# Cross attention and its hand-over to the expert layer: the last output products in four banks, the first two experts' weights prepared early, and the first expert started by halves

## The chip, the cores and the metric

The kernel runs on one NeuronCore of one Trainium2 chip. The metric is the device time of one execution in microseconds; given are the median of three timed runs and one execution under the hardware profiler. The engines are PE (matrix products and transposes), DVE (vector), ACT (scalar, activation functions), POOL (GpSimd) and SP, which here only issues DMAs.

## The reference, cut to what matters

Two decoder layers on x of shape (4, 256, 256). The change lies in the last two of six steps: cross attention of layer 1 and its mixture of experts.

```
x = x + _L1_xattn_ref(_layernorm(x), ctx, Wq, Wk, Wv, Wo, q_norm_w, k_norm_w, pos, itok)   # 16 heads, 4 key heads, 128 wide
    probs = softmax(q @ k.T * SCALE); attn = probs @ v; return attn.reshape(.., 16 * 128) @ Wo.T
x = x + _L1_ffn_ref(_layernorm(x), w_gate, wi_0, wi_1, wo)                                 # 8 experts, top 2, M = 128
    inter = silu(xf @ wi_0[e]) * (xf @ wi_1[e]); out = inter @ wo[e], weighted by softmax of the two top logits
```

## The kernel before, in words

Every stage is a block of five programs, one for each engine, written out in full and tied together by semaphores. Between stages all engines meet at a barrier (L68), which also clears the stage's semaphores.

**Cross attention** (`cross_stream`) is one long stream. A group g is one batch row and one key head with its four query heads; there are 16 groups (`GROUPS`), and each has 30 slots (`STEPS`), one for each tile of 128 keys and each half of the 512 query columns. In a slot PE computes the scores of one such tile (`score`, L1866, three bf16 products of the high and low halves of q and k), DVE adds the row shift and takes them out of the bank (`lower`, L2096), ACT takes the exponential (L1939), POOL adds it into `acc` for the softmax sum (L2033), and PE multiplies it with v two slots later (`weigh`, L1879, f32). The scores use banks 0 and 1 in turn, the weighted sums banks 2 and 3. Projections of the groups to come, maxima of scores (`piece`), and transposes fill the rest of the slots. In the last group, which has no successor, only the chain just named is left.

What is left of a group when its 30 slots are over is done in the slots of the next: ACT and DVE split the weighted sums into a bf16 high and low half (`att`, L1983 and L2138), PE sums `acc` over the partitions by a product with ones (`side` of kind "sum", L1895, in two halves of four columns of bank 6), DVE takes the reciprocals (L2149), and for each of the four heads PE makes the output product (`project_out`, L1905, six products of 128x256 into bank 6) and DVE scales it and adds it to x (`add_out`, L2159, two instructions). `sides_in` and `outs_in` are the tables that say in which slot each of these comes, and `bank6_before` says how many readers of bank 6 a writer has to wait for. Since all of them share bank 6, each product waits for the additions before it. `SLOTS` runs 14 slots past the last group, in which only this tail is left.

**The experts** (`expert_ffn`, tiles named `moe_...`) begin after the barrier. DVE normalises x (L86 to L2289, with a power on POOL, L2270), PE transposes it in four batches (L2391), ACT copies each out twice (bf16 high half L2354, f32 L2355), DVE makes the low half (L2294). PE then makes the up products of expert 0 in two halves n of 512 tokens (`up`, L2404, 24 instructions), the gate's logits (L2412), and then for each expert the next one's up products and this one's down products (L2426). The weights come in four pairs of experts by DMA into f32 tiles; ACT makes the high halves (`pair_high`, L2346 and L2347), POOL the low halves (`pair_rest`, L2266 and L2267).

`ctx_t` and `in_t` are the f32 context of one batch row and its two bf16 halves; they are allocated in `decoder` under the name `row0` (in the trace `row_ctx_t`, `row_in_t_hi`, `row_in_t_lo`). The last context row is loaded into `ctx_t`, and split, during group 10; `in_t` is read by the projections of keys and values until those of group 15 are made.

## Time and profile before

| | |
|---|---|
| median of 3 runs (lowest, highest) | 1791.28 us (1777.04, 1791.42) |
| the profiled execution, its time | 1775.8 us |
| its span, first to last instruction | 1774.0 us |
| mean granted clock of PE | 0.952 of full speed |
| busy: PE, DVE, ACT, POOL | 1585.2, 1334.4, 783.6, 1166.7 us |

The stages lie in the span as follows: cross attention's stream from 447.6 to 1676.2 us, the experts from 1677.5 us to the end. A busy share is time in which an engine works on some instruction, so the shares of several engines overlap. The granted clock is what PE's throttle allowed: 1.00 is 2.4 GHz, 0.50 is 1.2 GHz, and a value in between is a stretch that holds both.

### The profile page before, as it was taken

Reading aid. Unit: us, or ns where it says so; the run is one execution under the profiler, and the core shown is the slowest. Engines: PE = TensorE matmul, PEld = TensorE weight load, DVE = VectorE, ACT = ScalarE, POOL = GpSimd, SP = SyncE. Lnnn points to the kernel's source line nnn. Section 1 sums busy time; section 2 is a strip of 40 time slices with the busy share of each in tenths; the row PEclk is TensorE's granted clock in tenths of the full one; section 3 lists DMA queues with packets and bytes.
Section 4 is the critical chain, followed back from the end, with each engine's and each line's share of the span. In section 5 each row is a group of like instructions: output and inputs, shape, how many; then the busy total and the mean of one; then the engine's idle time right before and its main releaser. Section 6 shows DMA issues by size and latency. Waiting matters only on the chain. (4 is left out here: it accounts for less than half of the span.)

```text
span 1774.0 us, 26948 instructions
## 1 busy us (share of the span) xinstructions
PE 1585.2 (89%) x8690; PEld 912.3 (51%) x8690; DVE 1334.4 (75%) x2674; ACT 783.6 (44%) x1915; POOL 1166.7 (66%) x1088
## 2 busy tenths in 40 slices
PE   7697795776779999999999999899999999999797
PEld 4475463533534555554555555455555555544344
DVE  7675567778777888889788787877878778776454
ACT  2363564652435444443545444444444444433242
POOL 3663560132657799787779978678987787866442
PEclk9799897988989999999999999999999999999789
DMA  2001821010100000100000100000000000000110
GB/s 71 1 2 44 271 81 48 1 68 0 50 0 13 1 13 1 50 1 1 1 1 1 38 1 1 1 1 1 1 1 1 1 1 1 1 1 1 35 37 25
DMA packets 28530, 38.55 MB, mean 22 GB/s; under 512 B 4836, under 2 KB 24808, under 8 KB 28392
## 3 DMA queue, kind: packets, MB, share of 16 engines
q1 hardware_dynamic: 28392, 36.83, 6.3%
q8 instruction: 72, 1.18, 0.3%
q14 instruction: 66, 0.54, 0.1%
HBM read 35.78 MB, written 1.05 MB: 21 GB/s over the span
## 5 line engine op out<-in xcount | busy, mean ns | idle before, releaser
L2033 POOL TENSOR_TENSOR stream_acc<-stream_acc,stream_p 128x512 f32<-128x512 f32 x448 | 571.9, 1281 | 181.3 <-ACT stream_p L1939 180.0
L1939 ACT ACTIVATE stream_p<-stream_lowered 128x512 f32<-128x512 f32 (+1 forms) x480 | 302.7, 631 | 632.6 <-DVE stream_lowered L2096 596.4
L1879 PE MATMUL stream_banks<-stream_p,stream_v 128*128 128x512 f32 (+1 forms) x960 | 490.7, 593 | 4.5 <-ACT stream_p L1939 4.5
L2096 DVE TENSOR_TENSOR stream_lowered<-stream_banks,stream_shift_all 128x512 f32<-128x512 f32 (+1 forms) x480 | 329.2, 686 | 105.9 <-PE stream_banks L1866 93.1
L2103 DVE TENSOR_REDUCE stream_tops<-stream_banks 128x1 f32<-128x512 f32 (+1 forms) x512 | 324.4, 636 | 93.5 <-PE stream_banks L1852 92.4
L1879 PEld LDWEIGHTS stream_banks<-stream_p,stream_v 128*128 128x128 f32 (+1 forms) x960 | 182.5, 191 | 75.8 <-ACT stream_p L1939 7.0
L1852 PE MATMUL stream_banks<-stream_k_t_hi,stream_q_t_hi 128*128 128x512 bf16 (+1 forms) x512 | 185.4, 363 | 20.6 <-DVE stream_tops L2103 19.5
L1866 PE MATMUL stream_banks<-stream_q_t_hi,stream_k_t_hi 128*128 128x512 bf16 (+1 forms) x480 | 183.6, 382 | 0.0
L1866 PE MATMUL stream_banks<-stream_q_t_hi,stream_k_t_lo 128*128 128x512 bf16 (+1 forms) x480 | 182.6, 380 | 0.0
L1866 PE MATMUL stream_banks<-stream_q_t_lo,stream_k_t_hi 128*128 128x512 bf16 (+1 forms) x480 | 182.6, 380 | 0.0
L2040 POOL TENSOR_TENSOR stream_by_cos<-stream_by_cos,stream_by_sin 128x256 f32<-128x256 f32 x192 | 133.5, 718 | 35.0 <-DVE stream_by_sin L2129 34.9
L1852 PEld LDWEIGHTS stream_banks<-stream_k_t_hi,stream_q_t_hi 128*128 128x128 bf16 x512 | 50.1, 98 | 157.5 <-issue 154.8
L1949 ACT ACTIVATE stream_squares<-stream_banks 128x128 bf16<-128x128 f32 x368 | 95.4, 267 | 26.1 <-PE stream_banks L1798 26.1
L2046 POOL TENSOR_TENSOR stream_rms<-stream_var,cross_half 128x4 f32<-128x4 f32 x96 | 105.6, 1100 | 0.0
L2051 POOL TENSOR_TENSOR stream_normed<-stream_by_cos,stream_rms 128x512 f32<-128x512 f32 x96 | 97.2, 1012 | 11.3 <-PE stream_banks L1840 3.9
L1798 PEld LDWEIGHTS stream_banks<-early_w_kv_hi,row_in_t_hi 128*128 128x128 bf16 x416 | 40.7, 98 | 81.5 <-issue 56.8
L1798 PE MATMUL stream_banks<-early_w_kv_hi,row_in_t_hi 128*128 128x256 bf16 x416 | 80.3, 275 | 2.3 <-DVE stream_by_sin L2129 2.3
L1798 PE MATMUL stream_banks<-early_w_kv_hi,row_in_t_lo 128*128 128x256 bf16 x416 | 80.4, 275 | 0.0
L1798 PE MATMUL stream_banks<-early_w_kv_lo,row_in_t_hi 128*128 128x256 bf16 x416 | 80.4, 275 | 0.0
L1866 PEld LDWEIGHTS stream_banks<-stream_q_t_hi,stream_k_t_lo 128*128 128x128 bf16 (+1 forms) x480 | 47.5, 99 | 56.7 <-issue 0.8
L1949 ACT ACTIVATION_READ_ACCUMULATOR stream_squares<-stream_banks 128x1 f32 x368 | 73.4, 199 | 0.0
L2159 DVE SCALAR_TENSOR_TENSOR model_x<-stream_banks,stream_inv,model_x 128x256 f32<-128x256 f32 x128 | 56.0, 478 | 21.6 <-PE stream_banks L1905 21.6
(403 smaller groups left out, 2900.1 us busy)
## 6 DMA issues: line engine op xcount, KB each, us to landing
memory_raw_t<-in_ctx_t SPq DMA_DIRECT2D x4, 1601.0 KB, 8.1
row_ctx_t<-in_ctx_t SPq DMA_DIRECT2D x4, 1601.0 KB, 7.4
memory_raw<-in_ctx SPq DMA_DIRECT2D x4, 1536.0 KB
early_raw<-in_L_xattn_Wq SPq DMA_DIRECT2D x4, 512.0 KB, 3.9
stream_raw_o<-in_L_xattn_Wo SPq DMA_DIRECT2D x4, 512.0 KB, 3.7
moe_raw_up<-in_L_ffn_wi SPq DMA_DIRECT2D x8, 256.0 KB, 4.6
model_x<-in_x SPq DMA_DIRECT2D x1, 1024.0 KB, 5.5
ffn_raw_fc<-in_L_ffn_w_fc SPq DMA_DIRECT2D x1, 1024.0 KB, 5.0
```

What stands on the lines that cost most here:

```text
L1798: last = nc.tensor.matmul(out, rows, moving(two, c), start=(n == 0), stop=(n == 3 * DC - 1))
L1852: nc.tensor.matmul(ps[:, piece_bank(item), 0:n], q_t[0][:, g % 3, h, q * P:(q + 1) * P], k_t[0][:, g % 2, s:s + n], start=True, stop=True) ...
L1866: last = nc.tensor.matmul(ps[0:r, step % 2, :], k_t[one][:, g % 2, t * P:t * P + r], q_t[two][:, g % 3, 2 * n:2 * n + 2, :], start=(one == ...
L1879: nc.tensor.matmul(ps[:, 2 + n, :], v[0:r, g % 2, t, :], p32[0:r, step % 4, :], start=(t == 0), stop=(t == KT - 1)).then_inc(weighed, 1)
L1939: nc.scalar.activation(p32[0:r, step % 4, :], lowered[0:r, step % 3, :], ACT.Exp, scale=SCALE).then_inc(p32_ready, 1)
L1949: last = nc.scalar.activation(squares[:, h, :], heads[:, h - some.start, :], ACT.Square, accum_out=ss[:, u % 2, h:h + 1])
L2033: nc.gpsimd.tensor_tensor(acc[0:r, g % 2, cols], acc[0:r, g % 2, cols], p32[0:r, step % 4, :], ALU.add).then_inc(acc_ready, 1)
L2040: last = nc.gpsimd.tensor_tensor(by_cos[:, u % 2, 0:n, to], by_cos[:, u % 2, 0:n, to], by_sin[:, u % 2, 0:n, of], ALU.add)
L2046: nc.gpsimd.tensor_tensor(rms[:, u % 2, 0:n], var[:, u % 2, 0:n], half[:, 0:n], ALU.pow).then_inc(rms_ready, 1)
L2051: nc.gpsimd.tensor_tensor(normed[:, 0:n], by_cos[:, u % 2, 0:n], bcast(rms[:, u % 2, 0:n], 2, HD), ALU.mult).then_inc(normed_ready, 1)
L2096: nc.vector.tensor_tensor(lowered[0:r, step % 3, :], ps[0:r, step % 2, :], shift_all[0:r, g % 2, n * HALF:(n + 1) * HALF], ALU.add).then_i ...
L2103: nc.vector.tensor_reduce(tops[:, i, c:c + 1], ps[:, piece_bank(item), 0:CHUNKS[c][1]], AX_X, ALU.max).then_inc(piece_taken, 1)
```

## The change

Three things are changed.

1. **The tail of cross attention.** After the last group the four output products go to banks 4, 5, 7 and 0 (`out_bank`) instead of bank 6, so that they no longer wait for each other's additions, only once for the ends of all projections, pieces and score readings. The tables place them in slots 3, 4, 6 and 7 after the group's end (before: 5, 7, 10, 12), and the second half of the sums in slot 5 (before: 3), behind the first two products.
2. **The first pair of experts.** Their three DMAs are issued by SP within cross attention, once the last context row has been split, into the first 1536 columns of `ctx_t` (`first_pair`). In slot 8 of the last group ACT makes the high half in one instruction of 128x1536 into `in_t[0]`, and in slots 12, 15 and 18 DVE makes the low half in three of 128x512 into `in_t[1]`. `expert_ffn` runs inside the allocation of `row0` and reads experts 0 and 1 from there (`up_weights`, `down_weights`); `pair_high(0)` and `pair_rest(0)` are gone, and the gate's weights are loaded first.
3. **Expert 0 by halves.** Its first 12 up products wait for the low halves of batches 0 and 1 alone, the other 12 for all four.

```diff
-        found += {2: [("sum", g - 1, 0)], 3: [("sum", g - 1, 1)]}.get(late, [])
+        found += {2: [("sum", g - 1, 0)], 3 if g < GROUPS else 5: [("sum", g - 1, 1)]}.get(late, [])
...
-        return {5: [(g - 1, 0)], 7: [(g - 1, 1)], 10: [(g - 1, 2)], 12: [(g - 1, 3)]}.get(late, [])
+        first, second, third, last = (5, 7, 10, 12) if g < GROUPS else (3, 4, 6, 7)
+        return {first: [(g - 1, 0)], second: [(g - 1, 1)], third: [(g - 1, 2)], last: [(g - 1, 3)]}.get(late, [])
...
+        def out_bank(g, n):
+
+            return 6 if g < GROUPS - 1 else (4, 5, 7, 0)[n]
...
+                sp.wait_ge(ctx_ready, NCH * (BATCH - 1))
+                for i in range(2):
+                    sp.dma_start(raw_ups[i], experts[f"wi_{i}"][0:2].rearrange("e (c p) m -> p e c m", p=P)).then_inc(pair_loaded, 16)
+                sp.dma_start(raw_down, experts["wo"][0:2].rearrange("e p n -> p e n")).then_inc(pair_loaded, 16)
...
                 def project_out(g, n):
-                    wait_bank(("out", g, n))
+                    if g < GROUPS - 1:
+                        wait_bank(("out", g, n))
+                    else:
+                        pe.wait_ge(taken, len(parts))
+                        pe.wait_ge(piece_taken, len(piece_at))
+                        pe.wait_ge(lowered_ready, ALL)
...
+                    if g == GROUPS - 1 and late == 8:
+                        ac.wait_ge(pair_loaded, 48)
+                        ac.wait_ge(projected, len(parts))
+                        nc.scalar.copy(in_t[0][:].rearrange("p c n -> p (c n)")[:, 0:1536],
+                                       ctx_t[:].rearrange("p c n -> p (c n)")[:, 0:1536]).then_inc(pair_hi, 1)
...
+                    if g == GROUPS - 1 and late in (12, 15, 18):
+                        some = slice(512 * (late // 3 - 4), 512 * (late // 3 - 3))
+                        ve.wait_ge(pair_hi, 1)
+                        nc.vector.tensor_tensor(in_t[1][:].rearrange("p c n -> p (c n)")[:, some], ctx_t[:].rearrange("p c n -> p (c n)")[:, some],
+                                                in_t[0][:].rearrange("p c n -> p (c n)")[:, some], ALU.subtract).then_inc(pair_lo, 1)
...
-                pair_rest(0)
                 pair_rest(1)
...
-                pair_high(0)
...
-                pe.wait_ge(xnt_lo, BATCH)
...
-                        if e >= 1:
+                        if e == 0:
+                            pe.wait_ge(xnt_lo, 2 * n + 2)
+                        else:
                             pe.wait_ge(inner_ready, 2 * e - 1 + n)
...
+def first_pair(tile):
+
+    flat = tile.rearrange("p c n -> p (c n)")
+    ups = [flat[:, i * 512:(i + 1) * 512].rearrange("p (e c m) -> p e c m", e=2, c=DC) for i in range(2)]
+    return ups, flat[:, 1024:1536].rearrange("p (e n) -> p e n", e=2)
```

On DVE, at the end of the stream, this stands in a row before (from the last readings of scores; `model_x` is x):

```order
L2096 TENSOR_TENSOR stream_lowered<-stream_banks,stream_shift_all 128x512 x15
L2096 TENSOR_TENSOR stream_lowered<-stream_banks,stream_shift_all 65x512 x2
L2138 TENSOR_TENSOR stream_att_lo<-stream_banks,stream_att_hi 128x512 x2
L2149 RECIPROCAL stream_inv<-stream_banks 128x4 x2
L2159 SCALAR_TENSOR_TENSOR model_x<-stream_banks,stream_inv,model_x 128x256 x8
L1766 UNCONDITIONAL_BRANCH
L2282 UNCONDITIONAL_BRANCH
L86 BN_STATS moe_stats<-model_x 128x6 x8
```

and now, with its line numbers of the changed kernel:

```order
L2206 TENSOR_TENSOR row_in_t_lo<-row_ctx_t,row_in_t_hi 128x512
L2118 TENSOR_TENSOR stream_lowered<-stream_banks,stream_shift_all 128x512 x9
L2118 TENSOR_TENSOR stream_lowered<-stream_banks,stream_shift_all 65x512 x2
L2160 TENSOR_TENSOR stream_att_lo<-stream_banks,stream_att_hi 128x512 x2
L2171 RECIPROCAL stream_inv<-stream_banks 128x4
L2181 SCALAR_TENSOR_TENSOR model_x<-stream_banks,stream_inv,model_x 128x256 x4
L2171 RECIPROCAL stream_inv<-stream_banks 128x4
L2181 SCALAR_TENSOR_TENSOR model_x<-stream_banks,stream_inv,model_x 128x256 x4
```

The second reciprocal has moved behind the first four additions, and the third of the new subtractions stands among the readings of scores. PE follows the same pattern: the sums were one run of eight, and are now two of four with twelve output products between them.

On ACT, from the end of the stream to the first copies of the experts' stage, this stands before:

```order
L1939 ACTIVATE stream_p<-stream_lowered 128x512 x26
L1939 ACTIVATE stream_p<-stream_lowered 65x512 x2
L1983 CAST stream_att_hi<-stream_banks 128x512 x2
L1766 UNCONDITIONAL_BRANCH
L2340 UNCONDITIONAL_BRANCH
L2346 CAST moe_w_up_hi<-moe_raw_up 128x512 x2
L2347 CAST moe_w_down_hi<-moe_raw_down 128x512
L2354 CAST moe_xn_t_hi<-moe_banks 128x2x256
L2355 COPY moe_xn_t<-moe_banks 128x2x256
```

and now:

```order
L1956 ACTIVATE stream_p<-stream_lowered 128x512 x7
L2024 CAST row_in_t_hi<-row_ctx_t 128x1536
L1956 ACTIVATE stream_p<-stream_lowered 128x512 x19
L1956 ACTIVATE stream_p<-stream_lowered 65x512 x2
L2000 CAST stream_att_hi<-stream_banks 128x512 x2
L1774 UNCONDITIONAL_BRANCH
L2373 UNCONDITIONAL_BRANCH
L2386 CAST moe_xn_t_hi<-moe_banks 128x2x256
L2387 COPY moe_xn_t<-moe_banks 128x2x256
```

The three conversions of the first pair have become one, among the exponentials of the last group.

On POOL this stands before, behind the barrier:

```order
L2258 MEMSET moe_half 128x8
L2270 TENSOR_TENSOR moe_rs<-moe_rs,moe_half 128x8
L2266 TENSOR_TENSOR moe_w_up_lo<-moe_raw_up,moe_w_up_hi 128x512 x2
L2267 TENSOR_TENSOR moe_w_down_lo<-moe_raw_down,moe_w_down_hi 128x512
L2266 TENSOR_TENSOR moe_w_up_lo<-moe_raw_up,moe_w_up_hi 128x512 x2
L2267 TENSOR_TENSOR moe_w_down_lo<-moe_raw_down,moe_w_down_hi 128x512
L2277 TENSOR_TENSOR moe_inner_lo<-moe_inner,moe_inner_hi 128x512 x2
```

and now:

```order
L2292 MEMSET moe_half 128x8
L2304 TENSOR_TENSOR moe_rs<-moe_rs,moe_half 128x8
L2300 TENSOR_TENSOR moe_w_up_lo<-moe_raw_up,moe_w_up_hi 128x512 x2
L2301 TENSOR_TENSOR moe_w_down_lo<-moe_raw_down,moe_w_down_hi 128x512
L2310 TENSOR_TENSOR moe_inner_lo<-moe_inner,moe_inner_hi 128x512 x2
```

The subtractions of the first pair are gone from POOL; those that are left there are the second pair's, which wait for ACT's conversions of it.

## Rows read from the trace of the kernel before

**Rows 1.** The page, busy time and share of the span of each engine.

```profile
PE 1585.2 (89%) x8690; PEld 912.3 (51%) x8690; DVE 1334.4 (75%) x2674; ACT 783.6 (44%) x1915; POOL 1166.7 (66%) x1088
```

**Rows 2.** Timeline of DVE, end of the stream: start, duration, engine, line, operation [idle before].

```profile
1663.44 0.17 DVE L2149 RECIPROCAL stream_inv<-stream_banks 128x4 f32<-128x4 f32 x1
1665.66 0.18 DVE L2149 RECIPROCAL stream_inv<-stream_banks 128x4 f32<-128x4 f32 x1 [2.05 <-PE stream_banks L1895]
1667.48 0.87 DVE L2159 SCALAR_TENSOR_TENSOR model_x<-stream_banks,stream_inv,model_x 128x256 f32<-128x256 f32 x2 [1.63 <-PE stream_banks L1905]
...
1675.29 0.87 DVE L2159 SCALAR_TENSOR_TENSOR model_x<-stream_banks,stream_inv,model_x 128x256 f32<-128x256 f32 x2 [1.73 <-PE stream_banks L1905]
1677.50 2.71 DVE L86 BATCH_NORM_STATS2 moe_stats<-model_x 128x6 f32<-128x256 f32 x8 [1.33 <-PEq L68]
```

**Rows 3.** Timeline of PE, end of the stream.

```profile
1662.02 0.95 PE L1895 MATMUL stream_banks<-cross_ones,stream_acc 128*128 128x1 f32 x8
1663.72 1.84 PE L1895 MATMUL stream_banks<-cross_ones,stream_acc 128*128 128x1 f32 x8 [0.75 <-issue]
1665.95 0.37 PE L1905 MATMUL stream_banks<-cross_w_o_hi,stream_att_hi 128*128 128x256 bf16 x1 [0.39 <-issue]
```

**Rows 4.** Timeline of PE, first and last of six output products within the last group.

```profile
1630.38 0.27 PE L1905 MATMUL stream_banks<-cross_w_o_hi,stream_att_hi 128*128 128x256 bf16 x1
...
1630.92 0.27 PE L1905 MATMUL stream_banks<-cross_w_o_hi,stream_att_lo 128*128 128x256 bf16 x1
```

**Rows 5.** Busy time by stretch; the number before the last two is PE's granted clock.

```profile
1663.00:1664.00 1.00, 0.28 (x2) 0.31 (x2) 0.62 (x2) 0.00 (x0) 0.00 (x0) 0.77 0.00 0
```

**Rows 6.** Chain of waits, start of the experts: start, duration, engine, tile, line.

```profile
1682.92 4.37 DVE moe_xn L2289 x8
...
1687.33 1.13 PE moe_banks L2391 x4
...
1689.59 0.70 DVE moe_xn_t_lo L2294
...
1690.34 7.27 PE moe_banks L2404 x24
```

**Rows 7.** The normalising instructions of both stages (ns min/median/max), and POOL's timeline beside the second.

```profile
L1634 DVE TENSOR_SCALAR cross_w_row<-model_x,cross_w_mean_var,cross_w_rs x8: 407/410/414, 441.3 to 443.6; 128x256 f32<-128x256 f32 x8
L2289 DVE TENSOR_SCALAR moe_xn<-model_x,moe_mean_var,moe_rs x8: 403/406/1252, 1682.9 to 1686.0; 128x256 f32<-128x256 f32 x8
1684.62 2.50 POOL L2266 TENSOR_TENSOR moe_w_up_lo<-moe_raw_up,moe_w_up_hi 128x512 bf16<-128x512 f32 x2 [1.74 <-ACT moe_w_down_hi L2347]
```

**Rows 8.** Timeline of ACT, second copy of the experts' batch 1.

```profile
1686.30 0.62 ACT L2355 COPY moe_xn_t<-moe_banks 128x512 f32<-128x512 f32 x1
```

**Rows 9.** Busy time and granted clock by stretch, transposes of cross attention and experts.

```profile
444.00:445.00 1.00, 1.00 (x7) 1.00 (x6) 0.86 (x2) 0.62 (x2) 0.00 (x0) 0.51 0.00 0
445.00:446.00 1.00, 0.45 (x4) 0.21 (x2) 0.84 (x2) 1.00 (x2) 0.00 (x0) 1.00 0.00 0
...
1694.00:1695.00 1.00, 1.00 (x5) 0.45 (x4) 0.00 (x0) 0.00 (x0) 0.00 (x0) 0.87 0.00 0
...
1697.60:1701.00 3.40, 3.40 (x34) 3.40 (x33) 0.69 (x1) 3.34 (x7) 1.07 (x1) 1.00 0.00 0
1701.00:1704.00 3.00, 3.00 (x9) 1.09 (x9) 2.71 (x27) 1.68 (x3) 3.00 (x4) 0.51 0.00 0
```

**Rows 10.** Timeline of DVE and ACT, one slot of the last group.

```profile
1656.63 0.69 DVE L2096 TENSOR_TENSOR stream_lowered<-stream_banks,stream_shift_all 128x512 f32<-128x512 f32 x1 [0.81 <-PE stream_banks L1866]
1657.35 0.63 ACT L1939 ACTIVATE stream_p<-stream_lowered 128x512 f32<-128x512 f32 x1 [0.88 <-DVE stream_lowered L2096]
```

**Rows 11.** Conversions and subtractions of the same kind earlier in the stream (ns min/median/max).

```profile
L2006 ACT CAST cross_w_o_hi<-stream_raw_o x4: 1027/1028/1029, 531.4 to 755.2; 128x1024 bf16<-128x1024 f32 x4
L2184 DVE TENSOR_TENSOR cross_w_o_lo<-stream_raw_o,cross_w_o_hi x8: 919/1281/1789, 556.0 to 787.5; 128x512 bf16<-128x512 f32 x8
L2202 DVE TENSOR_TENSOR row_in_t_lo<-row_ctx_t,row_in_t_hi x12: 915/1280/1759, 640.9 to 1280.3; 128x1024 bf16<-128x1024 f32 x6, 128x512 bf16<-128x512 f32 x3, 128x642 bf16<-128x642 f32 x3
```

47 lines of the change are left out of this document (27 added, 20 removed).

## The prediction

> **What bounds the kernel now.** Read the page's busy shares first: PE works for 89% of the span, DVE for 75% [rows 1]. Over the stream PE is the bound, and nothing in this change takes a product from it there. So the question is where PE waits for others, and that is at the two ends that the change touches. The timelines of DVE and PE over the last 14 us of the stream come next [rows 2, 3]. The reader should see a relay: six output products, then two additions of 0.87 us for the pair, then six products again. The first pair of additions starts at 1667.48 and the fourth at 1675.29, so one round takes (1675.29 - 1667.48) / 3 = 2.60 us, of which DVE is idle 1.73. The second half of the sums starts only 0.75 us after the first has ended, since its bank has to be read first, and from about 1663.5 on the granted clock is at its lower level: the stretch from 1663 to 1664 has a mean of 0.77 [rows 5], and eight passes of the sums take 1.84 us instead of 0.95 [rows 3]. Last the chain of waits at the start of the experts [rows 6]: normalising until 1687.29, transposes until 1688.46, copies and the fourth subtraction until 1690.29, and only then, at 1690.34, the first up product. All of this lies in a row behind x, so what is taken from it comes off the end.
>
> **Term 1, the tail of cross attention.** Nothing is removed; the same 24 products, eight additions and two reciprocals are made, but the products have four banks. The waits that they get instead (all projections taken, all pieces taken, all scores read) are long over, as DVE's last reading of scores is three instructions ahead of the reciprocal. On PE the first product can follow the first sums, which end at 1662.97 [rows 3]. At full clock the starts of six products within the group are (1630.92 - 1630.38) / 5 = 0.108 us apart and the last takes 0.27, so one head takes 0.81 us and the next can start 0.65 after it [rows 4]. That gives heads 0 and 1 done at 1663.9 and 1664.5, the second sums (0.95 us) at 1665.3, heads 2 and 3 at 1666.1 and 1666.7. DVE is now the slower one: from 1663.95 it has four pairs of 0.87 and one reciprocal of 0.18 [rows 2], together 3.66, and I add 0.4 for the handing over between them. The last addition ends at 1668.0 instead of 1675.29 + 0.87 = 1676.16: **8.2 us less**. If the clock falls at 1663.5 as before, products are 0.21 us apart (the first one of the round shows 0.37 instead of 0.27 [rows 3, 4]) and the sums take 1.84; heads end at about 1664.1, 1665.4, 1668.5 and 1669.8, the last additions at 1670.75: 5.4 us less. I take the full clock, because the idle 0.75 us just ahead of the fall disappears and dense products stand there instead. The two ends are 5.4 and 8.4 (nothing for handing over but 0.2). The barrier behind it, 1.33 us [rows 2], stays.
>
> **Term 2, the start of expert 0.** Three things move its first product.
> Halves: the first 12 products need batches 0 and 1 alone. PE is free when its transposes end at 1687.33 + 1.13 = 1688.46 [rows 6]. That alone would give 1690.34 - 1688.5 = 1.85.
> POOL's subtractions of the first pair are gone. Of the eight normalising instructions most take 406 ns (busy, each overlapping the next), but the longest 1252, and they were under way while POOL subtracted from 1684.62 on; in cross attention, where POOL has nothing to do at that point, the same eight take 407 to 414 and the last starts 2.3 us after the first, against 3.1 [rows 7]. So normalising ends at 1682.92 + 2.7 = 1685.6 instead of 1687.29. What is late next is ACT, whose two copies for batch 1 end at 1686.30 + 0.62 = 1686.92 [rows 8]; the subtraction of 0.70 us [rows 6] then ends at 1687.65. PE's sixteen transposes, begun at about 1683.7 when two normalised rows are there, end by my estimate near 1687.4. So the first up product starts at 1687.7: 1690.34 - 1687.7 = **2.6 us less**, with 1.85 as the lower end. The second 12 need all four batches, which are there at about 1689.6, before the first 12 are done. ACT loses three conversions and the DMA wait ahead of them, and has the copies as early as PE allows; worth nothing more.
> The page GPSIMD Engine Reference of the Trainium skill (Specifications) says that GpSimd shares its SBUF interfaces with VectorE and contends with some forms of vector instruction, those with two SBUF inputs among them; the 1252 ns agree, but that same rule speaks against moving the work under POOL's accumulation, which is weighed in term 4.
>
> **Term 3, the clock in expert 0.** Before, it rises at about 1694.1 (mean of the stretch 0.87 [rows 9]), 3.8 us after the first up product, while PE had two gaps before it. Now PE works from 1683.7 on with one gap of about 0.3 us. In cross attention's head the same sixteen transposes, without a gap, were followed by the full clock at 445.0, 2.9 us after their start at 442.1 (0.51, then 1.00 [rows 9]). So the rise can come from 1686.6, which saves half of the 3.8 us, 1.9, to as late as before relative to the products, which saves nothing. I take the middle, **1.0 us less**. Further on the clock falls at 1701.0, after 3.4 us of the gate's small products, and stays low to about 1704.5 [rows 9]; if its rhythm shifts so that it doesn't fall, that is another 1.7 us, which I leave to the range.
> The page TensorE: Matmul & The Clock Gate (Part 4: PE-mode transpose) says that the full clock does not engage for transposes. By that rule this term would be nil and the sum smaller by 1.0; the stretch from 442 to 446 speaks against it.
>
> **Term 4, what is added to the last group.** SP issues three DMAs of 256 KB when the last context row is split, which happens at about 1282 [rows 11]; nothing stands behind them on SP's queue, and they are needed 340 us later. ACT converts 1536 columns in one go: 1024 take 1.03 us [rows 11] and 512 take some 0.6, so 1.45. ACT is idle 0.88 us in each slot of 1.50 [rows 10], so one exponential comes 0.57 late and the next on time. DVE subtracts three times 128x512, both inputs in SBUF and POOL at work beside it: 0.92 to 1.79 us each [rows 11], with 0.81 idle in each slot [rows 10], so a reading of scores comes 0.1 to 1.0 late. Behind both stands PE: it wants the bank back two slots later, and the exponential is multiplied two slots after its score. Reading takes 0.69 of the two slots, so I estimate the room at about 1.4 us, more than 1.0. **Nothing**, with all of it hidden; without that cover it would cost up to 1.45 + 3 x 1.79 = 6.8 us.
>
> **The sum.** 8.2 + 2.6 + 1.0 = 11.8 us less. Against the profiled execution's 1775.8 that is 1764.0. The median of the runs, 1791.28, lies 15.5 above the profiled time; the runs lie at two places, 1791.28 and 1791.42, and 1777.04 with the profiled one beside it, and the trace shows the lower place alone. Taken off the median it is **1779.5**. The smallest gain is 5.4 + 1.85 = 7.25, the largest 8.4 + 2.6 + 1.9 + 1.7 = 14.6.
>
> **The rivals.**
> (a) *The runs' two places.* If two of three runs of the changed kernel fall to the lower place, the median is 1777.04 - 11.8 = 1765.2, with the same mechanism. For it: half of the four times known lie there. Against: the median before lies at the upper. 0.32.
> (b) *The clock stays low in the tail and ACT and PE eat the rest*: 7.25 less, 1784.0. For it: small products alone brought it down at 1701 too [rows 9], without a gap. 0.12.
> (c) *Transposes don't raise the clock*: 10.8 less, 1780.5. It is the page's rule above as a mechanism here; against it the stretch at 445 [rows 9]. 0.10.
> (d) *The tail doesn't overlap.* If the products still run in turn with the additions, by a dependence that I overlook, only terms 2 and 3 remain: 1787.7. Against: banks, sums and reciprocals are all ready. 0.04.
> (e) *Slower: the splits starve PE in the last group.* Place: slots 8 to 18. If the room is less than DVE's delay, each of the four instructions holds PE for its length, 6.8 us, and each gap may bring the lower clock as the 0.75 us did at 1663, for some 3.5 us as from 1701 to 1704.5, costing half of it: 4 x 1.75 = 7.0. Together 13.8 against 11.8 gained: 1793.3. It decides only where a reading of scores comes over 1.4 us late. 0.04.
>
> **How the numbers follow.** The forecast has 0.38, the rivals 0.62 together. About 1% (18 us) is what a measurement of this kernel can tell from no change. Only (a) lies below 1773.4, so faster by over 1% has 0.33 (0.01 for more than I count), slower by over 1% 0.02, within 1% 0.65. The forecast's own range is 1776.7 to 1784.0. The range of all reaches from 1791.28 to the lower place with the largest gain, 1777.04 - 14.6 = 1762.4, at one end, and past (b) and (d) at the other, to 1788; (e) is left out.
>
> **What would show it.** In the tail: additions in two runs of four (about 1.8 us each) with the reciprocal between, the last ending near 1668.0 (1670.8 if the clock fell); products in a row with no wait for additions; granted clock from 1663.5 on. At the experts: eight normalising instructions in 2.7 us, all near 406 ns; first up product 10.2 us after the start of the statistics instead of 12.84; clock rising no later than 3.8 us after it. In the last group: PE without idle time in slots 8 to 18. The prediction is wrong if PE has gaps there, if heads wait for additions, or if the median changes its place by itself.

## The result, and the profile after

The changed kernel takes 1766.08 us (median of 4 runs, 1765.71 to 1766.45), the one before 1789.26 beside it (4 runs, 1777.04 to 1791.42): ratio 0.9899, 95% interval 0.9851 to 0.9948. The profiled execution took 1765.71, its span is 1763.9, against 1775.8 and 1774.0. So the profile shows 10.1 us and the medians show 23.2 to 25.2. The two have to be explained apart, and the 10.1 come first. PE's work is as before [rows 1]:

```profile
PE 1581.4 (90%) x8690; PEld 910.3 (52%) x8690; DVE 1334.1 (76%) x2677; ACT 782.5 (44%) x1913; POOL 1163.0 (66%) x1085
```

The tail, on DVE's timeline of the changed kernel [rows 2]:

```profile
1663.90 0.17 DVE L2171 RECIPROCAL stream_inv<-stream_banks 128x4 f32<-128x4 f32 x1
1664.19 1.85 DVE L2181 SCALAR_TENSOR_TENSOR model_x<-stream_banks,stream_inv,model_x 128x256 f32<-128x256 f32 x4
1665.96 0.17 DVE L2171 RECIPROCAL stream_inv<-stream_banks 128x4 f32<-128x4 f32 x1
1666.31 1.85 DVE L2181 SCALAR_TENSOR_TENSOR model_x<-stream_banks,stream_inv,model_x 128x256 f32<-128x256 f32 x4 [0.18 <-PE stream_banks L1922]
1669.52 2.71 DVE L86 BATCH_NORM_STATS2 moe_stats<-model_x 128x6 f32<-128x256 f32 x8 [1.35 <-PEq L68]
```

The relay is gone: two runs of four additions, with 0.18 us of waiting in place of three times 1.73. PE's timeline of the same kernel shows why [rows 3]:

```profile
1662.47 0.95 PE L1907 MATMUL stream_banks<-cross_ones,stream_acc 128*128 128x1 f32 x8
1663.28 0.27 PE L1922 MATMUL stream_banks<-cross_w_o_hi,stream_att_hi 128*128 128x256 bf16 x1
...
1664.48 0.27 PE L1922 MATMUL stream_banks<-cross_w_o_hi,stream_att_lo 128*128 128x256 bf16 x1
1664.59 0.95 PE L1907 MATMUL stream_banks<-cross_ones,stream_acc 128*128 128x1 f32 x8
1665.40 0.27 PE L1922 MATMUL stream_banks<-cross_w_o_hi,stream_att_hi 128*128 128x256 bf16 x1
```

Twelve products stand 0.109 us apart between the two groups of sums, the second sums take 0.95 and not 1.84, and nothing is idle. The start of the experts, in the chain of waits of the changed kernel [rows 6], and its eight normalising instructions (ns min/median/max) [rows 7]:

```profile
1673.27 1.65 POOL moe_rs L2304
...
1674.94 0.75 DVE moe_xn L2322 x2
...
1675.73 1.13 PE moe_banks L2423 x4
...
1678.97 0.70 DVE moe_xn_t_lo L2327
...
1679.72 6.15 PE moe_banks L2437 x24
1685.87 4.39 PE moe_banks L2445 x32
1690.26 7.62 PE moe_banks L2437 x24
```

```profile
L2322 DVE TENSOR_SCALAR moe_xn<-model_x,moe_mean_var,moe_rs x8: 403/405/414, 1674.9 to 1677.2; 128x256 f32<-128x256 f32 x8
```

The first up product now waits for the second low part. It starts 1679.72 - 1669.52 = 10.20 us after the statistics, where it was 12.84. Last the clock: busy time by stretch, PE's granted clock third from the end [rows 5, 9].

```profile
1663.00:1664.00 1.00, 1.00 (x11) 0.93 (x11) 0.83 (x3) 0.26 (x1) 0.00 (x0) 1.00 0.00 0
1682.00:1687.00 5.00, 5.00 (x31) 3.05 (x29) 1.15 (x2) 1.89 (x5) 0.00 (x0) 1.00 0.00 0
1687.00:1689.00 2.00, 2.00 (x16) 2.00 (x17) 0.23 (x1) 2.00 (x5) 0.81 (x1) 0.80 0.00 0
1689.00:1694.00 5.00, 5.00 (x16) 2.52 (x17) 3.49 (x28) 2.60 (x4) 4.79 (x5) 0.50 0.00 0
```

It stays up where it fell before (0.77 at 1663), but falls in the router's small products, and is low for 6.8 us, until about 1695. Before, the clock was low for 3.4 us behind the router's products, from 1701.1 to 1704.5.

The account, in us. From the first subtraction of the last weighted sums to the end of the last addition it took 14.18 and takes 5.73: -8.45. First up product after the statistics: -2.64. Expert 0's up products 6.15 instead of 7.27: -1.12. Router's products 4.39 instead of 3.47: +0.92. Expert 1's up products 7.62 instead of 6.90: +0.72. And the tail begins 0.45 later in this profile. Together -10.12, which is the difference of the spans.

### The profile page after: what moved, and what is told of

The parts are those of the page before. It is cut to its first block and busy times, and to the rows that moved or that the text cites. A ratio compares the mean times of both kernels' runs of the same rounds, so it can differ in the third digit from the quotient of the medians.

```text
span 1763.9 us, 26944 instructions
## 1 busy us (share of the span) xinstructions
PE 1581.4 (90%) x8690; PEld 910.3 (52%) x8690; DVE 1334.1 (76%) x2677; ACT 782.5 (44%) x1913; POOL 1163.0 (66%) x1085
## 5 line engine op out<-in xcount | busy, mean ns | idle before, releaser
L2125 DVE TENSOR_REDUCE stream_tops<-stream_banks 128x1 f32<-128x512 f32 (+1 forms) x512 | 324.2, 636 | 92.9 <-PE stream_banks L1864 91.6
L1891 PEld LDWEIGHTS stream_banks<-stream_p,stream_v 128*128 128x128 f32 (+1 forms) x960 | 182.6, 191 | 75.7 <-ACT stream_p L1956 7.0
L1878 PE MATMUL stream_banks<-stream_q_t_hi,stream_k_t_lo 128*128 128x512 bf16 (+1 forms) x480 | 182.6, 380 | 0.0
L1878 PE MATMUL stream_banks<-stream_q_t_lo,stream_k_t_hi 128*128 128x512 bf16 (+1 forms) x480 | 182.6, 380 | 0.0
L1852 PEld LDWEIGHTS stream_banks<-model_ident,stream_normed 128*128 128x128 f32 x368 | 43.9, 141 | 49.2 <-POOL stream_normed L2073 39.1
```

Source lines behind the costliest of these rows:

```text
L1878: last = nc.tensor.matmul(ps[0:r, step % 2, :], k_t[one][:, g % 2, t * P:t * P + r], q_t[two][:, g % 3, 2 * n:2 * n + 2, :], start=(one == ...
L1891: nc.tensor.matmul(ps[:, 2 + n, :], v[0:r, g % 2, t, :], p32[0:r, step % 4, :], start=(t == 0), stop=(t == KT - 1)).then_inc(weighed, 1)
L2125: nc.vector.tensor_reduce(tops[:, i, c:c + 1], ps[:, piece_bank(item), 0:CHUNKS[c][1]], AX_X, ALU.max).then_inc(piece_taken, 1)
```

## The experiments

All times in this section that are counted "from the statistics" start at the first BATCH_NORM_STATS2 of the experts; "tail" runs from the first subtraction of the last weighted sums to the end of the last addition; "group" runs from the next-to-last group's first reciprocal to the last group's, which contains the added splits; "statistics to end" is the span, given to 0.1, less the start of the statistics. From the profiles of all kernels:

| kernel | span | tail | last low part ends | statistics to end | group |
|---|---|---|---|---|---|
| before | 1774.0 | 14.18 | 12.78 | 96.50 | 47.05 |
| e1_again (before) | 1785.1 | 14.20 | 12.10 | 95.62 | 47.05 |
| after | 1763.9 | 5.73 | 12.10 | 94.38 | 47.05 |
| e5_after_again (after) | 1772.9 | 5.73 | 12.10 | 91.54 | 47.05 |
| e2_tail | 1782.9 | 5.73 | 12.54 | 97.20 | 47.05 |
| e3_pair | 1787.2 | 14.17 | 12.10 | 93.93 | 47.05 |
| e4_halves | 1786.6 | 14.21 | 12.11 | 92.93 | 47.05 |
| e6_sums_first | 1762.0 | 9.63 | 12.10 | 91.49 | 47.05 |
| e7_two_banks | 1763.9 | 5.73 | 12.11 | 94.48 | 47.05 |
| e8_splits_at_once | 1767.7 | 5.73 | 12.10 | 91.58 | 51.07 |
| e9_no_pair | 1780.0 | 5.73 | 12.78 | 94.89 | 47.06 |
| e10_no_halves | 1780.9 | 5.74 | 12.10 | 95.26 | 47.06 |
| e11_root_by_scalar | 1760.0 | 5.73 | 10.79 | 90.63 | 47.05 |
| e12_gate_mixed | 1762.9 | 5.73 | 12.10 | 93.18 | 47.05 |

The span alone says little, as e1 shows; the parts repeat to 0.05 us, apart from the one in which the clock moves.

**e1, the kernel before once more.** No edit.

> The kernel before, unchanged, once more. What is open is why its runs lie at 1777.0 and at 1787 to 1791.4 us while four runs of the changed kernel lie within 1765.7 to 1766.5. If the spread belongs to the kernel as it stands (chance decides in each run where it falls), this one shows times at both places again, up to 14 us apart, and a ratio near 1. If it belonged to the earlier occasion only, all its runs lie within 3 us of each other, near 1777.

Measured: 1780.18 us median of 12 runs, 1772.61 to 1790.50, ratio 0.9984 [0.9947, 1.0020] to 35 runs of the kernel before taken beside it. So the same code, built again, has six runs at 1772.6 to 1777.3 and six at 1783.1 to 1790.5. Where the 11.1 us between the two profiled spans lie can be read in self attention. Groups of lines between 15 and 46 us (busy us, mean ns), first of the kernel before, then of e1:

```profile
L403 PE MATMUL self_banks<-self_w_v,self_kvin_t 128*128 128x256 f32 x20 | 5.7, 405 | 0.0
```

```profile
L403 PE MATMUL self_banks<-self_w_v,self_kvin_t 128*128 128x256 f32 x12 | 6.2, 674 | 0.0
```

The same projections take 674 ns instead of 405, and in the same 31 us only 12 of them are made where 20 were. Busy time and clock of PE by stretch seem to say that the granted clock is full in both, before and e1:

```profile
24.00:34.00 10.00, 10.00 (x42) 1.00 0.01 2
```

```profile
0.00:5.00 5.00, 0.00 (x0) 1.00 0.58 178
24.00:34.00 10.00, 10.00 (x20) 1.00 0.00 0
```

That is a trap of the view. The trace keeps a list of clock records, each with a start, a length and a level. Where no record stands, the view prints 1.00, as from 0 to 5 us, where PE has done nothing yet. The first record in the list of before is a rise to full at 14.89 us of the span; in the list of e1 it is a rise to full at 47.35 us. PE's products change their rate at just these times. In before the starts of the first transposes go from 0.213 to 0.110 us apart at 14.9; in e1 the projections, on its timeline, go from four in 2.08 us to four in 1.13:

```profile
41.48 2.08 PE L403 MATMUL self_banks<-self_w_v,self_kvin_t 128*128 128x256 f32 x4
48.45 1.13 PE L403 MATMUL self_banks<-self_w_qk,self_kvin_t 128*128 128x256 f32 x4
```

So the slow stretch is the lower clock, and what differs is when it first rises: 14.9 to 16.1 us into the span in seven of the fourteen profiles (before, after, e6, e7, e8, e11, e12), 47.4 to 48.6 us in the other seven. Why it rises so late in half of the executions isn't shown; the first transposes start at 11.96 and 12.02 us, and the code up to there is the same. The stage behind starts its context DMAs (L591) at 170.1 in before and at 182.6 in e1: 12.5 us, more than the whole difference of the spans. In all profiles these starts are 169.8 to 170.1 with the early rise and 182.4 to 183.4 with the late one. It has nothing to do with the edit, and every kernel with ten runs or more has runs at both places.
The Trainium skill (TensorE: Matmul & The Clock Gate, Part 1: The HAM clock gate, Seeing it yourself) warns that recorded clock events on trn2 have been observed to be unreliable. These rows don't bear that out: where a record exists it agrees with the rate of the products, and the stretch ahead of the first one has none.

e1 also bears on how the transposes stand to the clock. PE's timeline, and PE by stretch:

```profile
1695.70 3.87 PE L2391 MATMUL moe_banks<-model_ident,moe_xn 128*128 128x128 f32 x16 [8.46 <-DVE moe_xn L2289]
1701.87 0.38 PE L2404 MATMUL moe_banks<-moe_xn_t_hi,moe_w_up_hi 128*128 128x512 bf16 x1 [2.31 <-DVE moe_xn_t_lo L2294]
```

```profile
1696.00:1699.00 3.00, 3.00 (x15) 0.50 1.07 303
1699.00:1699.70 0.70, 0.56 (x3) 0.71 1.16 324
1699.70:1702.00 2.30, 0.13 (x1) 1.00 1.18 308
1703.00:1706.00 3.00, 3.00 (x8) 0.50 0.01 4
```

Sixteen transposes alone, behind 8.46 us of idleness, were followed by the full clock before any up product had started; the wait of 2.3 us behind them was followed by the lower one from about 1702.8. The Trainium skill (TensorE: Matmul & The Clock Gate, Part 4: PE-mode transpose) says that the full clock does not engage for transposes in transpose mode. These rows don't agree, if its rule is meant for fp32 transposes too: they are made by `nc.tensor.transpose`, and the trace names them MATMUL and doesn't show the mode.

**e2, the tail alone, e3, the early weights alone, e4, the halves alone.** The diff in its three parts; e2 has these hunks and no others:

```diff
-        found += {2: [("sum", g - 1, 0)], 3: [("sum", g - 1, 1)]}.get(late, [])
+        found += {2: [("sum", g - 1, 0)], 3 if g < GROUPS else 5: [("sum", g - 1, 1)]}.get(late, [])
...
+            return 6 if g < GROUPS - 1 else (4, 5, 7, 0)[n]
```

e3 is the changed kernel without those and with the one wait for all four low parts; e4 is the kernel before with

```diff
-                pe.wait_ge(xnt_lo, BATCH)
...
+                        if e == 0:
+                            pe.wait_ge(xnt_lo, 2 * n + 2)
```

> Only the tail of cross attention is changed: four banks, later second sums, tighter slots. My theory: the profiled span falls by the tail's gain alone, 8.2 to 8.5 us, to about 1765.6, and the start of the experts is as before (first up product 12.84 us after the statistics begin). Rival, the tail's gain needs the other parts (the clock falls in between): 5.4 us, 1768.6. If this part is what removes the upper place of the run times, its runs lie within 1 us of each other; if not, some lie 10 to 14 us higher.

> Only the first pair's weights are prepared early; the tail runs in bank 6 as before and expert 0 waits for all four batches. My theory: the eight normalising instructions take 2.7 us instead of 4.4, but the first up product still waits for the fourth batch's subtraction, so it comes only about 0.7 us earlier (12.1 us after the statistics begin instead of 12.84); with the clock up to 1.5 us, span 1771.8 to 1773.3. Rival, POOL's subtractions had nothing to do with the slow normalising: it stays at 4.4 us and nothing is gained. Rival, the splits starve PE in the last group: span above 1774.

> Only expert 0 starts by halves. My theory: its first up product starts when the transposes are done, 11.0 us after the statistics begin instead of 12.84, so 1.85 us are gained before the clock is counted; span 1771 to 1773. Rival, PE only waits elsewhere (the second half for the fourth batch): less than 0.5 us, span 1773.5 to 1774.

Measured: 1781.41, 1787.87 and 1782.40 us (12 runs each), ratios 0.9985 [0.9948, 1.0023], 1.0028 [0.9997, 1.0059] and 0.9987 [0.9952, 1.0021]: with two places 12 to 15 us apart, a median of twelve runs can't show parts of 2 to 8 us. All three profiles have the late rise of the clock, so the spans that were expected can't be read from them either. Within the lower place the runs show the tail: the four lowest of e2 (middle 1768.1) lie 8.0 below the twenty of the kernel before there (1776.1). The parts show in the profiles. e2's tail is 5.73, as in the whole change. e3's low parts end at 12.10 and its eight normalising instructions are done in 2.67 us, not 4.36. e4's first up product starts at about 11.1, not at 10.2. It waits for POOL, whose last subtraction of weights ends at 1704.74, 11.07 after the statistics.

In e2 the first up product came at about 12.6, where 12.84 was expected. What differs from before lies ahead of it, on ACT's timeline in e2, and in e9 below, which has the same tail:

```profile
1691.97 1.14 ACT L2357 CAST moe_w_up_hi<-moe_raw_up 128x512 bf16<-128x512 f32 x2 [12.52 <-DMA moe_raw_down<-in_L_ffn_wo]
```

```profile
1690.42 1.14 ACT L2357 CAST moe_w_up_hi<-moe_raw_up 128x512 bf16<-128x512 f32 x2 [11.55 <-DMA moe_raw_down<-in_L_ffn_wo]
```

In every kernel without the early weights SP issues these three DMAs behind the barrier, at -0.04, 0.37 and 0.92 us from the statistics, whatever the tail does, and ACT waits for them. It starts at 5.3 us in before and e9, 5.6 in e1, 5.8 in e4 and 6.3 in e2, so the landing varies by 1 us and the tail isn't its cause. The start decides two things. POOL follows 1.8 us later, and each normalising instruction that starts after POOL has begun takes 1.25 us instead of 0.41: two of them in before and e9 (all eight 4.36 us), one in e1 and e4 (3.52), none in e2 (2.67), where POOL begins at 8.08, when they are over. And in e2 ACT's copies for the low parts come behind its late conversions, so that the low parts end at 12.54 us from the statistics. POOL's subtractions end at 11.45 (1697.15). The tail's gain stays whole. From the statistics to the end e2 takes 0.7 us more than before, in a profile whose clock rises 12.1 us after the first transpose, not 10.5.

**e5, the changed kernel once more.** No edit.

> The changed kernel, once more. The traces so far show where the two places of the run times come from: at the upper one PE makes the projections of self attention at half rate from 16 to 44 us of the span, long before anything that was changed. If that is chance, this kernel has both places too, at about 1766 and 1778 to 1780, and its four runs at 1766 were luck. If the change removes the upper place, all its runs lie within 2 us of 1766. From the first subtraction of the last weighted sums to the end of the span I expect 101.5 us again (before: 112.0, and 111.2 in its repetition).

Measured: 1770.38 us median of 12, ratio 0.9947 [0.9911, 0.9983]; six runs at 1762.0 to 1766.1 and six at 1774.7 to 1780.9. So the changed kernel has both places too, and the four runs of the result all lay at the lower. Of the kernel before, 33 runs were taken beside it: 14 at the lower place (1772.1 to 1779.2, middle 1775.6) and 19 at the upper (1785.0 to 1800.4, middle 1790.2). The changed kernel's six and six have middles of 1765.5 and 1780.5, so the change is worth 10.1 us at the lower place and 9.7 at the upper. Its profile differs from the first one of the same kernel in self attention, where its clock rises at 47.4 us, and in one part behind: 91.54 from the statistics to the end, 2.84 less, so that from the first subtraction of the last weighted sums to the end it is 98.9 where 101.5 was expected. PE by stretch:

```profile
1692.00:1693.00 1.00, 1.00 (x5) 0.68 0.43 133
1693.00:1706.00 13.00, 13.00 (x78) 1.00 0.00 1
```

Here the clock rose once and didn't fall in the router's products.

**e6, the second sums in their old place.** The sums of the second half ahead of the output products, as before:

```diff
-        found += {2: [("sum", g - 1, 0)], 3 if g < GROUPS else 5: [("sum", g - 1, 1)]}.get(late, [])
+        found += {2: [("sum", g - 1, 0)], 3: [("sum", g - 1, 1)]}.get(late, [])
```

> The changed kernel with the second half of the sums back in slot 3, ahead of all output products; banks and their slots stay. My theory: the second sums then wait for the first reciprocal with PE idle for 0.75 us as before; every product comes 1.6 us later and DVE's additions with them: the tail is 1.1 us longer at full clock and 3.7 us longer if that gap brings the clock down, so 102.6 or 105.2 us from the first of the last subtractions to the end instead of 101.5. Rival, only the banks matter and the order of the sums is worth nothing: 101.5.

Measured: tail 9.63, 3.90 more. PE's timeline, and all engines by stretch:

```profile
1661.27 1.83 PE L1907 MATMUL stream_banks<-cross_ones,stream_acc 128*128 128x1 f32 x8 [0.75 <-issue]
1662.97 0.38 PE L1922 MATMUL stream_banks<-cross_w_o_hi,stream_att_hi 128*128 128x256 bf16 x1
...
1667.83 0.42 PE L1922 MATMUL stream_banks<-cross_w_o_hi,stream_att_lo 128*128 128x256 bf16 x1
```

```profile
1661.00:1662.00 1.00, 0.73 (x4) 0.76 (x4) 0.17 (x2) 0.00 (x0) 0.00 (x0) 0.64 0.00 0
1662.00:1666.00 4.00, 4.00 (x21) 3.13 (x21) 1.33 (x4) 0.00 (x0) 0.00 (x0) 0.50 0.00 0
```

The 0.75 us of idleness is back, the clock is down behind it, and the 24 products, dense as they are, stand 0.21 apart. So of the tail's 8.45 us, 4.55 come from the banks with their slots and 3.90 from where the second sums stand. In all five kernels with the second sums in their old place (before, e1, e3, e4, e6) the clock falls within 0.2 us of the end of this gap, in the nine others it stays up through the tail. Counted as the expectation was, from the first of the last subtractions to the end, e6 took 102.5: the 3.90 more and, against the first profile of the change, 2.9 less behind the statistics, where its clock didn't fall. (1766.35 us, 8 runs, ratio 0.9931 [0.9889, 0.9972]: no slower than the change by its runs, which can't tell 4 us.)

**e7, two banks in place of four.**

```diff
-            return 6 if g < GROUPS - 1 else (4, 5, 7, 0)[n]
+            return 6 if g < GROUPS - 1 else (4, 5, 4, 5)[n]
...
+                        if n >= 2:
+                            pe.wait_ge(added, QT * (REP * g + n - 1))
```

> The changed kernel with the last output products in two banks in turn (4 and 5), each waiting for the additions of the product before the last. My theory: DVE's additions (0.88 us for a pair, 0.93 with the handing over) are what the tail is paced by, and with two banks PE works on one head while DVE adds the other; the sums in between delay the third anyway. 0 to 0.4 us longer, 101.5 to 101.9 us from the first of the last subtractions to the end. Rival, four banks are needed: each of the last two heads then waits about 0.8 us more, 103 us.

Measured: tail 5.73, the same to 0.01 (1775.12 us, 10 runs, 0.9957 [0.9920, 0.9994]). DVE is the slower one of the two, as the prediction had it; PE is far enough ahead with two banks.

**e8, the added subtractions in one slot and twice over.** Two subtractions of 1536 columns in one slot, in place of three of 512 in three slots:

```diff
-                    if g == GROUPS - 1 and late in (12, 15, 18):
-                        some = slice(512 * (late // 3 - 4), 512 * (late // 3 - 3))
+                    for first_col in ((0, 1600) if g == GROUPS - 1 and late == 12 else ()):
+                        some = slice(0, 1536)
```

The second of the two writes from column 1600 on; it is extra work whose output nothing reads.

> The changed kernel with DVE's three subtractions of the first pair made as one of 1536 columns, and that done twice (the second time into columns that nobody reads), both in slot 12 of the last group: some 5 us of DVE at once instead of 3 times 1.3. It measures the room that I estimated at 1.4 us. My theory: the reading of scores comes about 4.2 us late, PE is idle for about 2.7 us once, and the group lasts 2.7 us longer (from reciprocal to reciprocal 49.8 us instead of the 47.05 of all traces so far), 1.7 more if the clock falls. Rival, the slots hide it all: 47.05.

Measured: group 51.07, 4.02 more (1773.85 us, 10 runs, 0.9964 [0.9926, 1.0003]). DVE's timeline, PE's, and the stretches:

```profile
1638.73 3.68 DVE L2206 TENSOR_TENSOR row_in_t_lo<-row_ctx_t,row_in_t_hi 128x1536 bf16<-128x1536 f32 x2
1642.33 1.27 DVE L2118 TENSOR_TENSOR stream_lowered<-stream_banks,stream_shift_all 128x512 f32<-128x512 f32 x2
```

```profile
1639.89 1.02 PE L1891 MATMUL stream_banks<-stream_p,stream_v 128*128 128x512 f32 x2
1643.07 0.55 PE L1878 MATMUL stream_banks<-stream_q_t_hi,stream_k_t_hi 128*128 128x512 bf16 x1 [2.16 <-DVE stream_lowered L2118]
```

```profile
1642.00:1644.00 2.00, 0.93 (x3) 0.43 (x4) 1.61 (x3) 0.96 (x2) 0.25 (x1) 0.79 0.00 0
1644.00:1646.00 2.00, 2.00 (x5) 0.69 (x4) 0.69 (x1) 0.90 (x2) 2.00 (x2) 0.50 0.00 0
```

The reading of scores came 1642.33 - 1638.73 = 3.60 us late and PE stood for 2.16, so the room was 1.44. The expectation had 4.2 late and 2.7 of idleness. PE then went on at the lower clock for 3.4 us, until about 1646.6, and the other 1.86 of the 4.02 lie there. The room can be read from the timelines too: without the subtractions the reading would have ended at 1638.73 + 0.69 = 1639.42, and PE, which waits for its bank, had work until 1640.91. In the changed kernel the three subtractions took 0.94, 0.68 and 1.52 us, and the latest reading came 0.86 late (at 1637.01, behind a subtraction begun at 1636.15). The group took 47.05 as in every kernel without them. The cover is real, and 1.44 is its size.

**e9, the change without the early weights, e10, the change without the halves.** e9 is e2 and e4 together; e10 is the changed kernel with

```diff
+                pe.wait_ge(xnt_lo, BATCH)
...
-                        if e == 0:
-                            pe.wait_ge(xnt_lo, 2 * n + 2)
```

> The changed kernel with the first two experts' weights again loaded and split in the experts' stage, as before (four banks and halves kept). With the tail alone the weights' DMA landed late: ScalarE's first copy of them started 6.3 us after the start of the statistics, and GpSimd's last subtraction ended 11.45 us after it. Theory (the halves pay only with the early weights, and the shorter tail makes the late weights later): the first up product starts about 11.5 us after the start of the statistics, released by GpSimd's subtraction and no more by VectorE, against 10.20 in the changed kernel; the tail stays at 5.73 us. Rival (halves are worth as much without the early weights): the first up product at 10.2 us.

> The changed kernel with the one wait for all four low parts put back ahead of expert 0's up products (four banks and early weights kept). Theory: the first up product starts 12.1 to 12.2 us after the start of the statistics, when the fourth low part ends, 1.95 us later than in the changed kernel, and the stretch from the statistics to the first act*up product is 15.6 us, as in the early weights alone (15.60), against 14.13 to 14.48. Rival (the clock makes up for it, since it rises about 5.5 us after the first transpose whatever products run): the up products start later but nearly all run at full clock, so that the stretch grows by 1.2 us only; then halves are worth 1.2 us and not 1.95. The sum of statistics to end tells the two apart only if the clock doesn't fall in the gate products.

Measured in e9 (1780.02 us, 4 runs, 0.9992 [0.9945, 1.0039]), on DVE's timeline and POOL's:

```profile
1690.53 4.36 DVE L2300 TENSOR_SCALAR moe_xn<-model_x,moe_mean_var,moe_rs 128x256 f32<-128x256 f32 x8 [1.83 <-POOL moe_rs L2281]
...
1694.70 1.20 POOL L2278 TENSOR_TENSOR moe_w_down_lo<-moe_raw_down,moe_w_down_hi 128x512 bf16<-128x512 f32 x1
```

The first up product in the records starts at 11.50; as one of the first two is missing there, the real one came some 0.4 earlier, at 11.1. It waited for DVE's second low part, which ended at 10.98, with PE's own transposes until 10.95, and not for POOL, which was done at 1695.90 - 1685.11 = 10.79. So the size is near the 11.5 that was expected and its cause isn't: the weights landed 1 us earlier than in e2, and it was the normalising, 4.36 us beside POOL's subtractions, that was late. In e10 (1774.45 us, 4 runs, 0.9960 [0.9902, 1.0019]) the fourth low part ends at 12.10 and the first recorded up product is at 12.56, again the second of its pair, so 12.1: the halves are worth 1.9. Its stretch to the first act*up product was 16.96 and not 15.60, since the clock rose only 8.7 us after the first transpose: neither theory had that, and no rival about a clock that makes up for it is borne out.

**e11, the row scale by square root and reciprocal.** A version that the chain of waits suggested, since 1.65 us of it are POOL's power:

```diff
-                nc.gpsimd.tensor_tensor(rs[:, 1, :], rs[:, 0, :], half[:], ALU.pow).then_inc(rs_done, 1)
...
+                link(nc.vector.reciprocal(rs[:, 2, :], rs[:, 1, :]))
...
+                ac.wait_ge(rs_ready, 1)
+                nc.scalar.activation(rs[:, 1, :], rs[:, 0, :], ACT.Sqrt).then_inc(rs_done, 1)
```

> The changed kernel with the experts' row scale made by ScalarE's square root and VectorE's reciprocal, as the stage ahead of cross attention makes it, and not by GpSimd's power. GpSimd's power takes 1.64 us, and from the start of it to the first normalised row pass 1.67 us; ScalarE idles 13.6 us ahead of its first copy. Theory: square root and reciprocal take together 0.5 to 0.8 us with their waits, so every later step starts 0.9 to 1.1 us earlier, the first up product 9.1 to 9.3 us after the start of the statistics, and the stretch to the first act*up product shrinks by 0.5 to 1.1 us (the clock may rise later by as much against the products). Rival (the table for the square root, 1.28 us where ScalarE loads one, is loaded only when the variance is there): no gain, first up product at 10.1 to 10.4 us.

Measured: 1769.95 us (4 runs, 0.9934 [0.9873, 0.9995]; two at 1761.83 and 1762.65, two at 1777.3 and 1777.5), span 1760.0, the shortest of all. ACT and DVE on the timeline:

```profile
1669.33 1.28 ACT L2379 ACT_TABLE_LOAD   x1 [6.22 <-PEq L68]
1673.00 0.21 ACT L2379 ACTIVATE moe_rs<-moe_rs 128x8 f32<-128x8 f32 x1 [2.39 <-DVE moe_rs L2314]
1673.24 0.20 DVE L2316 RECIPROCAL moe_rs<-moe_rs 128x8 f32<-128x8 f32 x1 [0.28 <-ACT moe_rs L2379]
```

The table was loaded 3.7 us ahead of its use, beside the statistics. The fourth low part ends at 10.79 instead of 12.10: 1.31 us gained, a little more than expected. From the statistics to the first act*up product it is 12.32 where the change has 14.43. From the statistics to the end it took 90.63, the least of all, though the clock fell once behind the router's products.

**e12, the router's products in two portions.**

```diff
                         last.then_inc(up_ready, 1)
+                        if e == 0:
+                            pe.wait_ge(gate_loaded, 32)
+                            for t in range(TILES // 2 * n, TILES // 2 * (n + 1)):
```

> The changed kernel with the router's 32 small products in two portions of 16, the first between the two halves of expert 0's up products, the second behind them, in place of 32 in one piece behind them. In the profiled run of the change the clock fell to 0.50 in these 32 products (4.39 us in place of 3.47) and was low for 2.5 us of expert 1's up products, in the second profile of the same kernel it did not fall there. Theory (the fall comes from the long stretch of small products): with two portions of 16 it doesn't fall, up(0), router and up(1) take 16.2 to 16.5 us together (before: 17.9 with a late rise; changed kernel 18.2 and 16.3). Rival (whether it falls is chance of the phase against the chip's own window): it falls in about every second profile whatever the order, and this one run may show either; two portions of 16 take 3.5 us together with the full clock.

Measured: 1765.02 us (4 runs, 0.9940 [0.9868, 1.0012]); 93.18 from the statistics to the end. PE's timeline and POOL's:

```profile
1683.39 1.85 PE L2444 MATMUL moe_banks<-moe_w_gate,moe_xn_t 128*128 128x8 f32 x16
1687.68 1.85 PE L2444 MATMUL moe_banks<-moe_w_gate,moe_xn_t 128*128 128x8 f32 x16
1695.92 0.27 PE L2461 MATMUL moe_banks<-row_in_t_hi,moe_inner_hi 128*128 128x256 bf16 x1 [1.20 <-POOL moe_inner_lo L2310]
...
1690.17 2.27 POOL L2300 TENSOR_TENSOR moe_w_up_lo<-moe_raw_up,moe_w_up_hi 128x512 bf16<-128x512 f32 x2 [15.06 <-ACT moe_w_down_hi L2380]
```

The clock stayed at 1.00 from 1682 on, but the second half of the up products starts 1.7 us later now, ACT's conversion of the next weights and POOL's subtractions stand ahead of the inner product's low part, and PE waits 1.20 and later 1.23 us for it and for DVE. That is some 1.6 us more than the 91.5 of the kernels without a fall, and 1.2 less than the 94.4 with one. From the first up product of expert 0 (some 0.4 ahead of the first recorded one) to the end of expert 1's it took 14.8; expected were 16.2 to 16.5, but the 16.3 given there for the second profile of the change is not what its trace shows, which is 14.5 (18.1 in the first). Whether the two portions kept the clock up can't be told from one run, as the following table shows. Times in us after the first transpose of the experts, read from stretches of 0.5 us:

| kernel | first recorded up product | clock full | router's products | clock low again |
|---|---|---|---|---|
| before | 6.6 | 10.5 | 13.7 to 17.2 | 17.4 to 20.8 |
| e1_again | 6.2 | 3.7 to 7.1, and 10.5 | 12.8 to 16.3 | 17.3 to 20.8 |
| e2_tail | 6.8 | 12.1 | 14.4 to 17.9 | 19.0 to 22.4 |
| e3_pair | 6.2 | 3.9 | 11.1 to 15.0 | 14.2 to 17.6 |
| e4_halves | 5.1 | 3.7 | 10.1 to 13.6 | 14.0 to 17.4 |
| after | 4.0 | 5.6 | 10.0 to 14.4 | 12.5 to 19.3 |
| e7_two_banks | 4.0 | 5.7 | 10.0 to 14.4 | 12.6 to 19.4 |
| e5, e6, e8 | 4.0 | 5.0 to 5.2 | 9.7 to 13.2 | not |
| e9_no_pair | 5.3 | 9.1 | 12.1 to 15.6 | 15.9 to 19.3 |
| e10_no_halves | 6.4 | 8.7 | 12.5 to 16.4 | 15.6 to 19.0 |
| e11_root_by_scalar | 4.2 | 3.2 | 9.2 to 12.7 | 13.5 to 16.9 |
| e12_gate_mixed | 4.4 | 5.8 | 7.5 to 13.5, two portions | not |

Five profiles with the same products in the same places (after, e5 to e8) fall into two kinds: 94.4 to 94.5 us from the statistics to the end with a fall, 91.5 to 91.6 without. What decides it lies outside the edit; that it is the chip's own rhythm against the program's is my reading and isn't shown. The two that fell are those with the later rise (5.6 and 5.7, against 5.0 to 5.2), and e12 has a late one too (5.8) and didn't fall, which speaks for its portions, with one profile.

## Why the prediction was right, and where it wasn't

**Term 1, the tail: right.** 8.2 forecast, 8.45 measured, and 5.73 or 5.74 of tail in each of the kernels that have the whole edit. On the time axis of before the last addition would end at 1667.7 where 1668.0 was forecast; the handing over was sized at 0.4 and cost less. That the clock would stay up because the idle 0.75 us goes was an argument; e6 put the idleness back and got the lower clock, 24 products 0.21 apart and 3.90 us. It gained 4.55, less than the lower end of the range (5.4), which had the second sums in their new place. Rivals (b) and (d) fall.

**Term 2, the start of expert 0: right in size, with one part of it chance.** 2.6 forecast, 2.64 measured, first up product at 10.20 as forecast. Halves are worth 1.9 (e10 against the change). The rest was put down to POOL beside DVE's normalising. That is borne out: 2.67 us without POOL's subtractions beside them (e3, and e2, where POOL begins later), 4.36 with (e9). But the profile of before was an unlucky one: e1, the same code, took 3.52, and its last low part ended at 12.10. Against e1 the term is only about 2.0. What matters is when the DMA lets ACT and POOL start, and the prediction took that time from one profile. That the halves lean on the early weights was not foreseen: without them they stop at 11.1, whether with the old tail (POOL's end, e4) or the new (DVE's, e9). Moving the weights away removed a bound that the other two would have met.

**Term 3, the clock: the saving right, the net wrong.** 1.0 forecast for expert 0's up products, 1.12 measured. (The stretch with 0.87 puts the rise before at 1694.26, not at 1694.1, so it came 3.9 us after the first up product; now it comes 1.65 after it.) But I had left the fall at the router's products where it was, or gone (the other 1.7). It came earlier, in the middle of them, and lasted 6.8 us instead of 3.4: 0.92 and 0.72 more. So the term came to +0.5 in this profile. In e5 it was 2.84 better, with no fall at all: 2.3 less than before, more than the middle and inside the bound of 1.9 + 1.7. This is the term of the sum that was mis-sized: a single value stood where two outcomes 2.9 us apart exist. Rival (c) falls by e1's rows: transposes alone were followed by the full clock.

**Term 4, the added splits: right.** Nothing forecast, nothing measured, the group is 47.05 with and without, and ACT's conversion took 1.46 us for the 1.45 forecast. The estimated room of 1.4 us was measured as 1.44 (e8), though the prediction doesn't say how it comes from two slots of 1.50 and a reading of 0.69, which leave 2.3; beyond it the mechanism of rival (e) does act, with its stall and the clock behind it (2.16 + 1.86). In the change each instruction stays inside.

**The sum:** 11.8 forecast, 10.1 in the profiles (1764.0 against 1765.7), by 0.5 of term 3 with the wrong sign where 1.0 stood with the right one, and a tail that began 0.45 later; terms 1 and 2 were 0.3 better.

**The step that failed is from there to the median:** "Taken off the median it is 1779.5". It kept the upper of the two places for the changed kernel. The result's four runs all lay at the lower, which is rival (a), forecast as 1765.2 and measured as 1766.08. The places belong to the clock's first rise in self attention and to chance: e1 had six and six of them, e5 six and six. With the twelve runs of e5 the change is worth 0.5% (ratio 0.9947) and within a place 9.7 to 10.1 us, which is what the first two profiles had said (10.1). Of the 23 us between the medians some 13 are luck of the draw. That half the runs lie at each place was in view (two of four known times), and the chances of the two cases, 0.38 and 0.32, were about even; the single number had to pick one.

## What to carry to other kernels

Before taking a gain off a median, look whether the runs form clusters and find in the traces which stage makes the difference; then compare the parts of the span that the edit touches, from mark to mark, where 0.05 us can be told although the totals scatter by 12 or more. Where the clock is in question, look at the distance between the starts of equal products: the view's 1.00 ahead of the first clock record means only that there is none. At a tail, an idle gap on TensorE can cost twice, once for itself and once for the lower clock behind it (0.75 us cost 3.9 here, 2.16 cost 4.0); it needn't, for in e12 gaps of 1.20 and 1.23 us were followed by no fall. And work moved under another engine's cover is free up to a room that can be worked out from the timeline: the slack of the next instruction that someone waits for.
